# A row maximum by VectorE's 32x32 transposes and two small TensorE transposes

## What is computed

```python
def block(x):                                   # x: (2, 2048, 256)
    n = layernorm(x)
    q, k, v = (n @ Wq + bq) / 16, n @ Wk + bk, n @ Wv + bv
    s = where(causal, q @ k.T, -inf)
    x = x + softmax(s) @ v @ Wo + bo
    h = layernorm(x)
    prev = h shifted down by one row, zeros first
    xr, xk = mu_r * h + (1 - mu_r) * prev, mu_k * h + (1 - mu_k) * prev
    return x + sigmoid(xr @ W_r.T) * (square(relu(xk @ W_k.T)) @ W_v.T)
```

## Time and profile before

| quantity | value |
|---|---|
| median of 3 runs | 369.13 us (368.93 to 369.26) |
| the profiled execution, whole | 369.37 us |
| its span in the profile | 367.5 us |
| TensorE busy | 355.4 us, 97% |
| VectorE busy | 255.5 us, 70% |
| ScalarE busy | 238.9 us, 65% |
| GpSimd busy | 208.8 us, 57% |
| mean granted TensorE clock | 0.999 of full speed |

### The profile page before, as it was taken

The page is one execution under the profiler, slowest core; times in us unless marked ns, Lnnn a source line. Parts: engine busy times, 40 slices in busy tenths (PEclk is TensorE's granted clock), DMA queues, the critical chain, the costliest instruction groups (busy, mean ns, idle before and its releaser), DMA issues.

```text
span 367.5 us, 6730 instructions
## 1 busy us (share of the span) xinstructions
PE 355.4 (97%) x2463; PEld 324.5 (88%) x2463; DVE 255.5 (70%) x561; ACT 238.9 (65%) x454; POOL 208.8 (57%) x238
## 2 busy tenths in 40 slices
PE   8999999999999999999999899999999999999985
PEld 6787888998999888799997789999999999999964
DVE  3679799597666886668169777768748588584455
ACT  2344536975697467696655763875657787788663
POOL 3011350767659454597745383626746599599951
PEclk9999999999999999999999999999999999999999
DMA  8600000000020003002000000200000000000001
GB/s 238 191 2 1 2 0 3 0 3 1 30 86 2 1 2 114 3 4 89 24 3 0 2 0 30 87 0 3 2 29 23 8 3 2 29 30 0 30 29 59
DMA packets 11938, 10.66 MB, mean 29 GB/s; under 512 B 1921, under 2 KB 11906, under 8 KB 11906
## 3 DMA queue, kind: packets, MB, share of 16 engines
q1 hardware_dynamic: 10544, 10.23, 8.8%
q10 hardware_dynamic: 1362, 0.01, 0.2%
HBM read 6.04 MB, written 4.19 MB: 28 GB/s over the span
## 4 chain that ended last, share of the span: by engine, by line
PE 79%; DVE 10%; POOL 5%; ACT 3%; issue 2%; ACTq 0%; DVEq 0%
PE W L725 16%; PE W L728 15%; PE W L729 15%; PE O L883 8%; PE O L885 8%; PE O L884 8%; PE W L759 3%; POOL mix_lo L331 2%; DVE mix L643 2%; DVE peak L600 1%; DVE x_in L621 1%; DVE stats L623 1%; PE O L908 1%; PE B L855 1%; PE B L864 1%
## 5 line engine op out<-in xcount | busy, mean ns | idle before, releaser
L325 POOL TENSOR_TENSOR p_lo<-st,p_hi 128x512 fp32r<-128x512 f32 (+1 forms) x79 | 90.7, 1166 | 49.1 <-ACT p_hi L372 48.6
L883 PE MATMUL O<-v_hi,p_hi 128*128 128x258 f32 x272 | 78.1, 287 | 0.0
L885 PE MATMUL O<-v_hi,p_lo 128*128 128x258 f32 x272 | 76.8, 282 | 0.0
L884 PE MATMUL O<-v_lo,p_hi 128*128 128x256 f32 x272 | 76.5, 281 | 0.0
L600 DVE TENSOR_TENSOR peak<-peak,W 128x512 f32<-128x512 f32 (+3 forms) x70 | 42.2, 602 | 43.1 <-ACT st L372 42.4
L372 ACT ACTIVATE st<-W 128x512 f32<-128x512 f32 (+1 forms) x79 | 42.0, 538 | 43.8 <-PE W L729 43.4
L728 PE MATMUL W<-xT_lo,kT_hi 128*128 128x512 f32 (+2 forms) x188 | 65.8, 350 | 0.0
L725 PE MATMUL W<-xT_hi,kT_hi 128*128 128x512 f32 (+2 forms) x188 | 64.7, 344 | 1.0 <-DVE v_lo L512 0.8
L729 PE MATMUL W<-xT_hi,kT_lo 128*128 128x512 f32 (+2 forms) x188 | 63.3, 336 | 0.0
L372 ACT ACTIVATE p_hi<-st 128x512 fp32r<-128x512 f32 (+1 forms) x79 | 45.5, 576 | 12.9 <-PE O L885 10.7
L408 ACT ACTIVATE st<-st 128x512 f32<-128x512 f32 (+1 forms) x79 | 44.9, 568 | 12.1 <-DVE st L612 12.0
(11 more groups left out here) (133 smaller groups left out, 771.6 us busy)
## 6 DMA issues: line engine op xcount, KB each, us to landing
out_dram<-gate SPq DMA_DIRECT2D x15, 256.0 KB, 2.2
x_in<-in_L_attn_y_all_dram SPq DMA_DIRECT2D x7, 512.0 KB, 4.1
x_in<-in_L_attn_y_all_dram SPq DMA_DIRECT2D x4, 128.0 KB, 3.7
h_row<-in_L_attn_Wk_dram SPq DMA_DIRECT2D x1, 256.0 KB, 3.3
h_row<-in_L_attn_Wq_dram SPq DMA_DIRECT2D x1, 256.0 KB, 3.7
st<-in_L_attn_Wv_dram SPq DMA_DIRECT2D x1, 256.0 KB, 3.9
st<-in_L_attn_Wo_dram SPq DMA_DIRECT2D x1, 256.0 KB, 4.4
mix<-in_L_ffn_W_k_dram SPq DMA_DIRECT2D x1, 256.0 KB, 5.6
```

The costliest lines, as they stand in the source:

```text
L325: g.tensor_tensor(p_lo[:, u % NP, r], score_tile(u), p_hi[:, u % NP, r].bitcast(f32), ALU.subtract)\
L883: mm(o[:, 0:VW], p_hi[:, u % NP, w], v_hi[:, j + b, :], start=j + b == 0, stop=False)
L884: mm(o[:, 0:C], p_hi[:, u % NP, w], v_lo[:, j + b, :], start=False, stop=False)
L885: last = mm(o[:, 0:VW], p_lo[:, u % NP, w], v_hi[:, j + b, :], start=False, stop=end)
```

## The change

The work of the two stages is cut into five, for each score group:

- `mt`, on VectorE: one instruction transposes every 32x32 block of `peak` (128x512) into bank `B`, and a reduction over each run of 32 gives `peak_32`, 128x16: on each partition the maximum over the 32 partitions of its own quarter. For J = 7 and 8 it is 128x8.
- `mr`, on TensorE: one transpose of `peak_32` into 16 (or 8) partitions of `B`.
- `mm`, on VectorE: a reduction over the four quarters, on those 16 partitions, read four times over so that the result `peak_all` is laid out for all four quarters.
- `ms`, on TensorE: one transpose of `peak_all`, back to 128x16 in `B`.
- `mb`, on VectorE: a copy of it to SBUF (`peak_col`), and one transpose of 32x32 blocks with the input broadcast, which writes the full 128x512 of maxima to `B` (two transposes of half the size for J = 7 and 8).

The first stage waits for the shifts of the group before on VectorE (`sub_done`), since it overwrites `B`. The four inner waits (`mt_ready`, `part_turned`, `all_turned`, `col_ready`) are all in VectorE's stream, `part_ready` and `all_ready` in TensorE's. All tables of slots are replaced by others, and three are new (`MR_AT`, `MM_AT`, `MS_AT`).

```diff
@@ tables (the others are changed in the same way)
-    PV_AT = [8, 8, 10, 10, 19, 19, 19, 20, 21, 22, 22, 24, 26, 26, 26, 27, 27, 27, 28, 28, 30, 31, 31, 31, 41, 41, 41, 42, 42, 43, 43, 43, 43, 43, 43, 44, 44, 44, 46, 46, 50, ...
-    MT_AT = [(4,), (13,), (24,), (40,), (44,), (53,), (65,), (71,), (109,)]
-    MB_AT = [(5,), (17,), (25,), (40,), (44,), (54,), (68,), (72,), (144,)]
-    MIX_AT = [(20, 21), (27, 30), (35, 39), (49, 49), (61, 63), (72, 72), (118, 129), (192, 200), (278, 283)]
+    PV_AT = [9, 15, 15, 15, 17, 17, 17, 19, 21, 22, 22, 24, 26, 26, 26, 27, 27, 28, 28, 28, 29, 29, 29, 30, 40, 40, 41, 42, 42, 42, 43, 43, 43, 44, 44, 44, 45, 46, 48, 48, 50, ...
+    MT_AT = [(3,), (11,), (23,), (39,), (43,), (51,), (64,), (70,), (100,)]
+    MB_AT = [(6,), (14,), (25,), (39,), (45,), (57,), (66,), (74,), (163,)]
+    MIX_AT = [(19, 19), (28, 28), (35, 35), (51, 53), (63, 65), (72, 72), (142, 150), (222, 232), (316, 347)]
+    MR_AT = [(5,), (13,), (24,), (39,), (44,), (53,), (65,), (71,), (138,)]
+    MM_AT = [(5,), (13,), (24,), (39,), (44,), (53,), (65,), (72,), (144,)]
+    MS_AT = [(6,), (14,), (25,), (39,), (45,), (55,), (66,), (73,), (151,)]
@@ buffers
-        peak_col = sb("peak_col", [P, 2, TG])
+        peak_32, peak_all, peak_col = sb("peak_32", [P, SQ]), sb("peak_all", [SQ, P]), sb("peak_col", [P, SQ])
@@ VectorE
+            def squares(J):
+                return SQ // WIDE[J], WIDE[J]
             def peak_part(J):
-                n = GROUPS[J][2]
+                n, w = squares(J)
+                dve.wait_ge(maxed, FIRST[J + 1])
+                if J > 0:
+                    dve.wait_ge(sub_done, FIRST[J])
+                turned = bank_b[:].rearrange("p (n w b) -> p w n b", n=n, w=w)
+                v.transpose(turned, peak[:, J % 2, :].rearrange("p (w n b) -> p w n b", w=w, n=n)).then_inc(mt_ready, 1)
                 dve.wait_ge(mt_ready, J + 1)
-                v.tensor_reduce(peak_col[:, J % 2, 0:n], bank_b[:].rearrange("p (t k) -> p t k", t=n),
-                                axis=AX.X, op=ALU.max).then_inc(peak_ready, 1)
+                v.tensor_reduce(peak_32[:, 0:n], bank_b[:].rearrange("p (n b) -> p n b", n=n), axis=AX.X, op=ALU.max)\
+                    .then_inc(part_ready, 1)
+            def whole_part(J):
+                n, w = squares(J)
+                dve.wait_ge(part_turned, J + 1)
+                rows = bank_b[0:n, 0:P].rearrange("n (g a) -> n a g", a=SIDE).unsqueeze(1).to_broadcast([n, P // SIDE, SIDE, P // SIDE])
+                v.tensor_reduce(peak_all[0:n, :].rearrange("n (r a) -> n r a", a=SIDE), rows, axis=AX.X, op=ALU.max).then_inc(all_ready, 1)
+            def spread_part(J):
+                n, w = squares(J)
+                dve.wait_ge(all_turned, J + 1)
+                v.tensor_copy(peak_col[:, 0:n], bank_b[:, 0:n]).then_inc(col_ready, 1)
+                dve.wait_ge(col_ready, J + 1)
+                for i in range(w):
+                    last = v.transpose(bank_b[:, i * n * SIDE:(i + 1) * n * SIDE].rearrange("p (n b) -> p n b", n=n),
+                                       peak_col[:, 0:n].unsqueeze(2).to_broadcast([P, n, SIDE]))
+                last.then_inc(mb_ready, 1)
@@ TensorE
-            def gather_peak(J):
...
-                        last = nc.tensor.transpose(bank_b[:, c * P:(c + 1) * P], peak[:, J % 2, (b * n + t) * P:(b * n + t + 1) * P], ident[:])
-            def spread_peak(J):
...
-                        last = nc.tensor.transpose(bank_b[:, c * P:(c + 1) * P], peak_col[:, J % 2, t:t + 1].to_broadcast([P, P]), ident[:])
+            def turn_part(J):
+                n = SQ // WIDE[J]
+                pe.wait_ge(part_ready, J + 1)
+                nc.tensor.transpose(bank_b[0:n, 0:P], peak_32[:, 0:n], ident[:]).then_inc(part_turned, 1)
+            def turn_all(J):
+                n = SQ // WIDE[J]
+                pe.wait_ge(all_ready, J + 1)
+                nc.tensor.transpose(bank_b[:, 0:n], peak_all[0:n, :], ident[0:n, 0:n]).then_inc(all_turned, 1)
```

58 lines of the change are left out of this document (25 added, 33 removed).

## The result

| | before | changed |
|---|---|---|
| median | 369.19 us (368.93 to 369.31) | 373.94 us (372.41 to 373.95, 4 runs) |
| ratio | | 1.0119, 95% interval 1.0093 to 1.0145 |
| span of the profiled execution | 367.5 us | 372.1 us |
| TensorE busy, instructions | 355.4 us, 2463 | 356.0 us, 2409 |
| VectorE busy | 255.5 us | 277.5 us |

The change makes the kernel slower by 1.2%. The prediction was 366.9, 0.6% faster. Three of the four runs, the profiled one among them, took 373.93 to 373.95 with a mean clock of 0.995; the fourth took 372.41 with 0.999, of which more at `e1_fill3`. In the tables that follow a median stands beside that of the kernel before on the same chip, 369.3 to 369.4 each time.

What follows compares the result with a forecast made beforehand. It took TensorE's own work (busy 97%) plus its stops as the bound. 369.4 - 4.9 + 3.4 - 0.7 + 1.4 + 1.1 - 2.5 = 367.2, by the median 366.9 us, 0.6% faster; range 363.9 to 371.4.

Steps and rivals of the forecast that it cites:

- The new order counted as relief alone: Between 196 and 213 us one stop of about 0.9 stays, relief -2.5; at 154.84 the stop of 0.7 goes, -0.7.
- untouched: The program's end: the same work follows the last `pv`, and the last group's exchange has 5.9 and 9.7 us of cover.
- By itself none of it is on the path: VectorE's added 17.6 us of work costs time only where TensorE or a first `pv` stands close behind.
- counted at nothing: The five groups other than 0 to 3: TensorE's other work covers the exchange's 2.4 and 6.0 us, so no cost.
- Removed and added on TensorE: 72 transposes removed save 8.1 us, 18 small ones at 0.18 add 3.2: saving 4.9 us, bounds 1.6 to 6.5.
- VectorE's operations: Per group two block transposes, a second reduction and a copy: 1.95 us, over nine groups 17.6 us more VectorE work.
- Rival 4: The block transpose is long: at 2.4 us the kernel takes 373.2, at 1.2 us 369.0; chance 0.06.
- Group 3: No cover: TensorE waits out the whole exchange between its last score block and both small transposes, +3.4 us (2.6 to 4.6).
- Groups 0 to 2: Group 0's first `pv` waits 1.7 instead of about 0.3, +1.4; groups 1 and 2 are close, +1.1 together.
- the second (the relief doesn't come, 369.4): The stops between 196 and 213 us move and stay, VectorE having 2 us more per group: 369.4, the same; chance 0.19.
- The third (VectorE sets the pace, 371.9): In the first three groups VectorE's idle time can't be filled, 7.5 us late instead of 2.5: 371.9, slower; chance 0.16.

Runs made afterwards that it cites:

- e1_fill3: The changed kernel with 11 more matmuls, result overwritten, filling TensorE's stop at group 3's two small transposes; 372.42 us, ratio 1.0085.
- e9_old_cover3: The operations of before in the changed kernel's tables, group 3's gather behind the `kk` products and its spread behind the `rr` products; 370.53 us, ratio 1.0031.
- e2_cover3: The changed kernel with group 3's first small transpose behind the `kk` products and its second behind the `rr` products; 370.47 us, ratio 1.0034.
- e6_load: The kernel before with three unread block transposes of 480 elements added on VectorE behind each group's reduction; 376.06 us, ratio 1.0181.
- e14_load_new: e9_old_cover3 with three unread block transposes of 480 elements added on VectorE behind each group's reduction; 375.86 us, ratio 1.0177.
- e4_old_order: The changed kernel's operations placed in the order (slot tables) of the kernel before; 390.98 us, ratio 1.0578.
- e5_early0: e2_cover3 with group 0's whole exchange one slot earlier; 374.52 us, ratio 1.0139.
- e8_all: e5_early0 with `h_row` written as `scalar_tensor_tensor` and the copy and second block transpose of groups 5 and 8 earlier; 384.36 us, ratio 1.0406.

## Why the prediction was wrong

The runs split the way from before to the changed kernel into three, and the prediction's terms can be put beside them. The split goes one way round; in the old order the new operations cost 21.7 us.

| step | runs | measured | predicted |
|---|---|---|---|
| the new order, group 3 covered, old operations | before to `e9_old_cover3` | +1.2 | -2.5 - 0.7 = -3.2 |
| the new operations in it | `e9_old_cover3` to `e2_cover3` | -0.1 | -4.9 + 1.4 + 1.1 = -2.4 |
| group 3 without cover | `e2_cover3` to changed | +3.5 | +3.4 |

By its own steps:

- **The new order counted as relief alone: the step that failed, by 4.4 us.** The sum has -2.5 at 196 to 213 us and -0.7 at 154.84 for it, and calls the end "untouched". Both stops went, as predicted; the three of the earlier trace rows and the wait of the earlier trace rows went whole, where 0.9 was to stay. But the order brings stops of its own, 1.09 at 71 us, 0.5 and 0.45 at 136 and 148, 0.47 at 22.8, 0.32 at group 8 and 1.18 for 0.71 near the end, and some 0.8 us in no stop. No term stood for any of them; they are there with the old operations too.
- **"By itself none of it is on the path": failed in part.** VectorE's work was to cost nothing but what the first three groups lose. Group 5's stop of 0.94 was "counted at nothing": the slot of the second small transpose was read there, not that of the copy behind it. Dead work has a price of 0.35 and 0.29 us for each us (`e6_load`, `e14_load_new`). All in all the new operations gave back the 4.2 us that they save, where the sum let 2.5 be given back.
- **Removed and added on TensorE: too good by 0.7.** The small transpose was priced at 0.18 from the pipelined row; the first of a group costs 0.11 or 0.26, the second 0.27. The range held it.
- **VectorE's operations: right in size.** Block transpose 0.72 for 0.68, copy 0.17 for 0.15, VectorE busy +18.9 by the new operations for +17.6. Rival 4 is out. The Trainium skill's sentence in "Vector Engine (DVE) Microarchitecture Reference", section 3.8, that a transpose sustains one element per cycle per lane, fits a transpose that lasts 0.72 beside 0.68 for a subtraction of the same size.
- **Group 3: right in the stop, right in the sum by luck.** Predicted stop 3.4 (its own parts add up to 3.3), measured 3.2. Its second half, 1.5 us of halved clock, was in no sum. The windows of the earlier trace rows show the clock full in every stretch of before; they also show no stop of that length, so they could not speak for one. The two come to 4.7; covering group 3 wins only 3.5, since the wait of 1.12 for `mix_lo` comes up in their place. That 3.5 lies so near to 3.4 is luck.
- **Groups 0 to 2: the sum is right, half of it by luck.** Group 0's first `pv` waits 1.24 for 1.4, by the chain that was counted. The 1.1 for groups 1 and 2 is not there; what stands in its place is 1.09 for `h_row` at 71 us, which the order makes.

The largest miss is thus in the order, 4.4 us; the new operations add 2.3, and group 3 0.1, together 6.8 of the 7.0 between 366.9 and 373.94; the runs of before beside which the experiments stand are 0.2 above the 369.13 of the forecast.

Of the rivals, the second (the relief doesn't come, 369.4) says that stops go and "new ones can take their place". That is what the order does, but its reason is wrong: the stops at 196 to 213 us did go, and the new ones stand elsewhere and don't need VectorE's extra work. The third (VectorE sets the pace, 371.9) put 5 us more into the first three groups, which is not there; that VectorE's work has a price the runs with dead work bear out. What stays open: where the rest of the order's 1.2 lies, the 1.4 us that the new operations cost outside of stops, and how much could be had back by tables planned anew for them.

## What to carry to other kernels

Price a new order in both directions: it takes stops away and makes others, and only a run of the old operations in the new order tells the two apart. An engine that is busy 70% of the time is not free: before pricing work on it at nothing, take a price from a run with dead work at the place (here 0.3 us for each us). Count a chain's cover from the last of its instructions, with what stands ahead of that one in its queue, and look at what stands behind an instruction that waits for another engine: work that was ready waits with it. A move to relieve one engine moves every queue that is tied to the same slot; moving the maximum's exchange a slot ahead cost 4 us by ScalarE's exponentials, without becoming any earlier. And a stop on TensorE of 3 us can cost more than itself.

## What the runs showed of the hardware

- **The clock behind a stop.** After 3.2 us of stop TensorE ran at 0.50 for about 3 us and lost 1.5. It fell too behind stops of 3.0 us in `e4_old_order` (0.53 from 200 to 206 us) and `e5_early0` (0.50 from 44 to 46), and behind one of 1.89 at 309.40 in `e4_old_order` (0.51 from 309.5 to 313; TensorE had been busy throughout from 296 to 307.5). But it doesn't fall each time: it stayed at 1.00 behind the stop of 2.98 in `e8_all` (44 to 46 us) and behind one of 1.83 at 58.36 in `e4_old_order` (58 to 62), and the changed kernel's fourth run kept a mean of 0.999. Behind the stops of up to 1.4 us in `e2_cover3` and `e14_load_new` the mean clock of the kernel stays at 1.0 and 0.999. What decides is not shown.
- **VectorE beside GpSimd.** `h_row` takes 0.41 us at the median and 1.0 when GpSimd writes low parts, as `tensor_scalar` and as `scalar_tensor_tensor` (0.49 and 1.1). Instructions that read a PSUM bank and one SBUF tile keep their 0.68 at the same time. The Trainium skill has the rule, "SBUF — State Buffer", section "SBUF: two separate sides": the two engines share a pair of ports by an exclusive lock, which a VectorE instruction takes in a two-port fast mode, or with two inputs from SBUF against a GpSimd instruction that reads SBUF. By that rule the `scalar_tensor_tensor` form of `h_row`, with two inputs from SBUF, is held up by `p_lo`, and `v_lo`, with one input from PSUM, isn't; the trace agrees with both (1.1 and 0.68 us). The `tensor_scalar` form would be held up if it runs in such a mode; no row names its mode, but it is held up as much (1.0).
- **TensorE as a transposer.** Four large transposes in a row cost 0.44 us. The small one that reads `peak_32` costs 0.11 in most places and 0.26 in two, the one that reads `peak_all` 0.26 to 0.27 everywhere. One small transpose is a quarter to 60% of four large ones; why the second is dearer, with fewer columns, is not shown.
